# A mixture-of-experts kernel on one core: the first chunk as eight plain products instead of seven products of sum forms

## The chip, the cores and the metric

The kernel runs on one core of a Trainium2 chip. The metric is device time in microseconds for one execution, and lower is better. Engines are named as in the profile: PE (TensorE, matrix products), DVE (VectorE), ACT (ScalarE), POOL (GpSimd) and SP (SyncE, which here only issues DMAs).

## The reference, cut to what matters

```python
# x: (16, 256, 256) float32;  Wg, Wu: (8, 256, 1024);  Wd: (8, 1024, 256);  Sg, Su, Sd: the shared expert
g = einsum('bsd,edf->ebsf', h, Wg);  u = einsum('bsd,edf->ebsf', h, Wu)
expert_outs   = einsum('ebsf,efd->ebsd', silu(g) * u, Wd)
expert_output = einsum('be,ebsd->bsd', gating_probs, expert_outs)
shared = einsum('bsf,fd->bsd', silu(h @ Sg) * (h @ Su), Sd)
out = x + (1 - sg) * expert_output + sg * shared
```

So there are nine experts (eight routed, one shared) over 4096 tokens of width 256, with a hidden width of 1024, all in float32.

## The kernel before, in words

**Tiles and groups.** The tokens are cut into 8 tiles of 512. Two tiles (t = 0 and 1) make a group, and there are four groups. For each group the kernel walks through 9 experts with 8 chunks of 128 hidden units each. `n` counts the chunks of the first group. The input of a group has four blocks: x[c][t], with c the half of the width and t the tile. A chunk has four weight blocks of 128x128: A11 and A12 (gate weights, first and second half of the width), A21 and A22 (up weights), and the down weights D0 and D1.

**Seven products instead of eight.** Gate and up for two tiles are a 2x2 times 2x2 block product, which takes eight block products if done plainly. The kernel makes it with seven, p1 to p7, from sums of weight blocks (S1 to S4) and sums of input blocks (T1 to T4). The raw slot of A21 is overwritten by S3. In the first group p1 opens the bank `chain_ps`, p6, p7 and p4 add to it, p5 and p3 use `p53_ps`, p2 uses `side_ps`. Between them ACT copies banks away ("taps": tap1, tap5, tap_u2) and DVE adds the taps to banks to form gate0, gate1 and up1; up0 is what p4 leaves in `chain_ps`. ACT then applies silu, and DVE multiplies silu, up and a coefficient to h0 and h1.

**hi and lo.** Each operand is split into hi (ACT casts it to the matmul's format) and lo (raw minus hi), and each product is three matmuls: hi by hi, hi by lo, lo by hi (`product`, L680 to L686). So one product is three rows of the trace, of lines L684, L685 and L686.

**The first group makes the weights.** In group 0, for each chunk, SP loads the raw blocks, POOL makes the sums (`weight_sums`, L457), ACT the hi part (`weight_hi`, L975), POOL the lo part (`weight_lo`, L480, 1152 columns), and SP stores both to DRAM (`keep_gate`, `keep_down`), from where the later groups fetch them. The down weights of two chunks also get sums (`pair_sums`, four additions, and `down_lo`). There are four raw slots: chunk 4 takes the slot of chunk 0, and ACT may write the hi part of chunk 4 only when the four stores of chunk 0 have landed (`kept_stored[0]`, L982).

**The order on the engines.** Each engine has one program, in order. For the first group, PE's is `first_units` (chunks 0 and 1, then the down product of chunk 0 for tile 1), and then `unit(e, k)` per chunk: p4 of the chunk before, p1, p5, down products of tile 0, p6, p2, p3, p7, down products of tile 1. That is 11 products. The other engines follow with units of their own. ACT's unit ends with both silus and, in the first expert, with the hi part of a chunk further on (`both_hi`: chunk 3 behind unit 1, chunk 4 behind unit 2, chunk 5 behind unit 3). At the head of its next unit stands the hi part of h1. POOL runs through `first_chunks` (L571) in a written order: the sums of chunks 1, 2 and 3, the lo parts of chunks 1 and 2, the pair sums, the lo part of chunk 3, the sums of chunk 4, `down_lo`, the lo part of chunk 4, the pair sums of 2 and 3, the sums of chunk 5. SP runs through `first_keeps` (L305).

**The opening of chunk 0.** In the kernel before, DVE makes the four sums of chunk 0 (`w_sum`, L1419) and the lo parts of its blocks and of all seven input forms (`first_forms`, L1402). ACT makes the hi parts in `first_unit` (L1148). Then `first_steps` (DVE) and `second_unit` (ACT) bring in chunk 1.

## Time and profile before

| quantity | us |
|---|---|
| median of 3 runs | 2104.42 |
| lowest, highest | 2104.19, 2104.86 |
| profiled execution, its own time | 2105.31 |
| its span (first to last instruction) | 2103.5 |
| PE busy | 2091.9 (99%) |
| POOL busy | 1611.3 (77%) |
| DVE busy | 1447.7 (69%) |
| ACT busy | 1304.2 (62%) |

The busy shares are means over the whole span. The change touches the first chunk only, which lies within the first 25 us or so. The later stages run the same instructions in both kernels.

### The profile page before, as it was taken

To read this page: it belongs to the slowest core of one execution; us is meant where nothing else is said; L and a number is where in the kernel's file an instruction comes from. 1 tells how busy PE (TensorE), PEld (TensorE's weight loads), DVE (VectorE), ACT (ScalarE), POOL (GpSimd) and SP (SyncE) were. 2 spreads that over 40 slices of the span, in tenths; PEclk is the share of its full clock that TensorE was granted. 3 is DMA by queue.
4 is the path that set the end of the run, shared out by engine and by line. 5 is a ranking of instruction groups with operands and counts; after the bars stand their busy time and mean duration, and the time that the engine had idled before them with its cause. 6 is when DMAs were issued, how large, how long until landed. Compare 5 with 4: busy or idle time off the path is not lost.

```text
span 2103.5 us, 33963 instructions
## 1 busy us (share of the span) xinstructions
PE 2091.9 (99%) x9183; PEld 1719.2 (82%) x9183; DVE 1447.7 (69%) x2630; ACT 1304.2 (62%) x2335; POOL 1611.3 (77%) x1442
## 2 busy tenths in 40 slices
PE   8999999999999999999999999999999999999999
PEld 6888888888888888888888888888888888888887
DVE  7666666666666666666676666666667666666666
ACT  7777777777566555555556655555555555555555
POOL 7988887877488777777778877777777778777776
PEclk9999999999999999999999999999999999999999
DMA  6976666666555455445445446445445445545443
GB/s 221 349 245 238 234 242 230 242 229 232 203 197 209 173 215 209 173 194 209 174 193 210 177 191 229 178 188 209 180 186 210 184 184 210 203 183 209 183 183 143
DMA packets 122747, 433.94 MB, mean 206 GB/s; under 512 B 13760, under 2 KB 41792, under 8 KB 122688
## 3 DMA queue, kind: packets, MB, share of 16 engines
q1 hardware_dynamic: 122688, 433.32, 54.9%
q8 instruction: 17, 0.28, 0.1%
q14 instruction: 42, 0.34, 0.0%
HBM read 329.85 MB, written 103.28 MB: 206 GB/s over the span
## 4 chain that ended last, share of the span: by engine, by line
PE 99%; DVE 1%; issue 0%; ACT 0%; DMA 0%; DVEq 0%; ACTq 0%
PE chain_ps L684 15%; PE chain_ps L685 15%; PE chain_ps L686 15%; PE down_ps L686 8%; PE down_ps L685 8%; PE down_ps L684 8%; PE p_ps L684 6%; PE p_ps L686 6%; PE p_ps L685 6%; PE side_ps L686 4%; PE side_ps L685 4%; PE side_ps L684 4%; DMA acc<-xT 0%; ACT h_forms L1089 0%; DVE acc L1232 0%
## 5 line engine op out<-in xcount | busy, mean ns | idle before, releaser
L455 POOL TENSOR_TENSOR h_forms<-h_t,h_forms 128x512 fp32r<-128x512 f32 x429 | 560.5, 1325 | 269.1 <-ACT h_forms L1089 269.1
L684 PE MATMUL chain_ps<-x_hi,gate_forms 128*128 128x512 f32 x1080 | 422.5, 391 | 0.2
L686 PE MATMUL chain_ps<-x_hi,gate_forms 128*128 128x512 f32 x1080 | 420.7, 390 | 0.0
L685 PE MATMUL chain_ps<-x_lo,gate_forms 128*128 128x512 f32 x1080 | 420.7, 390 | 0.0
L455 POOL TENSOR_TENSOR h_t<-h_b,h_t 128x512 f32<-128x512 f32 x214 | 312.1, 1458 | 73.5 <-DVE h_b L1226 58.2
L1232 DVE TENSOR_TENSOR p_ps<-tap_p,chain_ps 128x512 f32<-128x512 f32 x216 | 150.4, 696 | 247.5 <-PE chain_ps L686 247.5
L1103 ACT COPY chain_ps<-chain_ps 128x512 f32<-128x512 f32 x216 | 123.1, 570 | 281.6 <-DVE h_a L1226 193.9
L1089 ACT CAST h_forms<-h_t 128x512 fp32r<-128x512 f32 x429 | 267.3, 623 | 15.1 <-POOL h_t L455 3.6
L455 POOL TENSOR_TENSOR w_lo<-w_raw,w_hi 128x1152 fp32r<-128x1152 f32 (+2 forms) x74 | 191.9, 2594 | 78.1 <-ACT w_hi L984 77.6
L684 PEld LDWEIGHTS chain_ps<-x_hi,gate_forms 128*128 128x128 f32 x1080 | 202.5, 188 | 54.8 <-ACT chain_ps L1103 5.3
L686 PEld LDWEIGHTS chain_ps<-x_hi,gate_forms 128*128 128x128 f32 x1080 | 202.7, 188 | 43.2
L685 PEld LDWEIGHTS chain_ps<-x_lo,gate_forms 128*128 128x128 f32 x1080 | 202.8, 188 | 37.3
L1108 ACT ACTIVATE silu<-chain_ps 128x512 f32<-128x512 f32 x216 | 129.5, 599 | 161.7 <-PE chain_ps L686 161.7
L1232 DVE TENSOR_TENSOR silu<-tap_p,chain_ps 128x512 f32<-128x512 f32 x216 | 148.0, 685 | 80.2 <-PE chain_ps L686 80.2
L1089 ACT CAST h_forms<-h_b 128x512 fp32r<-128x512 f32 x214 | 134.2, 627 | 109.2 <-DVE h_b L1226 109.2
L1030 ACT COPY tap_p<-p_ps 128x512 f32<-128x512 f32 x288 | 170.7, 593 | 6.3
L455 POOL TENSOR_TENSOR h_t<-h_a 128x512 f32<-128x512 f32 x108 | 140.2, 1298 | 44.5 <-DVE h_a L1226 44.5
L1093 ACT ACTIVATE p_ps<-p_ps 128x512 f32<-128x512 f32 x216 | 125.7, 582 | 72.5 <-PE p_ps L686 72.4
L686 PE MATMUL down_ps<-h_forms,down_forms 128*128 128x512 f32 x433 | 168.7, 390 | 0.0
L684 PE MATMUL down_ps<-h_forms,down_forms 128*128 128x512 f32 x433 | 168.5, 389 | 0.0
L685 PE MATMUL down_ps<-h_forms,down_forms 128*128 128x512 f32 x433 | 168.5, 389 | 0.0
L684 PE MATMUL p_ps<-x_hi,gate_forms 128*128 128x512 f32 x432 | 168.2, 389 | 0.0
(117 smaller groups left out, 4878.0 us busy)
## 6 DMA issues: line engine op xcount, KB each, us to landing
gate_forms<-kept_gate SPq DMA_DIRECT2D x216, 896.0 KB, 7.4
down_forms<-kept_down SPq DMA_DIRECT2D x108, 896.0 KB, 4.6
kept_gate<-w_hi SPq DMA_DIRECT2D x72, 448.0 KB, 2.5
kept_gate<-w_lo SPq DMA_DIRECT2D x72, 448.0 KB, 3.1
w_raw<-w SPq DMA_DIRECT2D x72, 256.0 KB, 3.0
w_raw<-w SPq DMA_DIRECT2D x72, 128.0 KB, 2.8
kept_down<-d_hi SPq DMA_DIRECT2D x36, 256.0 KB, 2.3
kept_down<-d_lo SPq DMA_DIRECT2D x36, 256.0 KB, 2.8
```

The source lines that it names most:

```text
L455: return nc.gpsimd.tensor_tensor(dst, a, b, ALU.subtract)
L684: nc.tensor.matmul(bank, w_high, hi, start=start, stop=False, **on)
L685: nc.tensor.matmul(bank, w_high, lo, start=False, stop=False, **on)
L686: return nc.tensor.matmul(bank, w_low, hi, start=False, stop=stop, **on)
L1030: nc.scalar.copy(tap_p5[:], p53_ps[:]).then_inc(p5_tapped, 1)
L1089: nc.scalar.copy(h_forms[:, H_AT[form]], h_full[form][:] if full is None else full).then_inc(form_hi[form], 1)
L1093: nc.scalar.activation(p53_ps[:], p53_ps[:], ACT.Silu).then_inc(silu_done[1], 1)
L1103: nc.scalar.copy(chain_ps[:, 1 - k % 2, :], chain_ps[:, k % 2, :]).then_inc(p1_seeded, 1)
L1108: nc.scalar.activation(silu[:, 0], chain_ps[:, 1 - k % 2, :], ACT.Silu).then_inc(silu_done[0], 1)
L1232: return nc.vector.tensor_tensor(dst, a, b, ALU.add)
```

## The change

Chunk 0 is computed by eight plain products (`plain_chunk` on PE): gate0, up0, gate1 and up1 are each two products accumulated in one bank, in the order gate0, up0, gate1, up1 with the first half of the width, then gate1, up1, gate0, up0 with the second. Its gate and up come out of the banks directly, so chunk 0 has no taps and no additions, and ACT reads both silus from the banks. The fourth input block (x[0][1], called b12) gets a hi and a lo part of its own, in the place of a form of the second group. The sums S1 to S4 of chunk 0, which are still needed for the copies in DRAM, are made on POOL; their hi part (a DVE copy) and lo part (DVE) come at the end of DVE's `first_steps`. Chunk 1 is then the first with taps and forms. The lo part of chunk 1's A11 and A12 moves from POOL to DVE. POOL makes the coefficients before the lo part of chunk 1. SP's `first_keeps` loads chunk 5 first, then 6, then 4, and the store of chunk 0's down weights moves behind the loads of the down weights of chunks 4 and 5, which wait for the pair sums (`d_sums` 4).

```diff
-FIRST_X_HI = (B11, T1, B21, B22, T2, T3, T4)
+FIRST_X = (B11, B21, B22, T1, T2, T3, T4)
+PLAIN = 1
@@ SP, first_keeps
-                sp.wait_ge(w0_lo_done, 4)
-                load_blocks(0, 4)
-                sp.wait_ge(w_lo_done, 1)
-                load_blocks(0, 5)
-                keep_gate(0, 0)
-                keep_down(0, 0)
-                sp.wait_ge(w_lo_done, 2)
-                load_blocks(0, 6)
-                sp.wait_ge(w1_lo_done, 2)
+                sp.wait_ge(w_lo_done, 1)
+                sp.wait_ge(w1_gate_lo_done, 1)
+                load_blocks(0, 5)
+                sp.wait_ge(w_lo_done, 2)
+                load_blocks(0, 6)
+                sp.wait_ge(w0_lo_done, 4)
+                load_blocks(0, 4)
+                keep_gate(0, 0)
+                sp.wait_ge(w1_lo_done, 1)
                 sp.wait_ge(d_sums, 4)
                 load_down(0, 4)
                 load_down(0, 5)
+                keep_down(0, 0)
                 keep_gate(0, 1)
@@ POOL
             def first_chunks():
+                plain_chunk_sums()
                 next_sums(0, 0)
-                pool.wait_ge(w1_hi_done, 1)
-                part_lo(1, A11, A12).then_inc(w1_lo_done, 1)
+                coefficients()
                 pool.wait_ge(w_hi_done, 1)
                 part_lo(1, S3, S4).then_inc(w_lo_done, 1)
-                coefficients()
                 next_sums(0, 1)
                 next_sums(0, 2)
+                pool.wait_ge(w_hi_done, 2)
+                part_lo(2, D0, A22)
                 pool.wait_ge(w_hi_done, 3)
-                part_lo(2, D0, A22)
+                part_lo(2, S1, S4).then_inc(w_lo_done, 1)
                 pool.wait_ge(w_hi_done, 4)
-                part_lo(2, S1, S4).then_inc(w_lo_done, 1)
                 part_lo(1, D0, D1).then_inc(w1_lo_done, 1)
                 pair_sums(0, 0)
@@ PE
+            def plain_chunk():
+                gate0, up0, gate1, up1 = chain_ps[:, 1, :], chain_ps[:, 0, :], p53_ps[:], side_ps[:]
+                first_w(0)
+                b11 = x_of(0, B11, True)
+                product(gate0, made(0, A11), b11, start=True, stop=False)
+                first_w(1)
+                product(up0, made(0, A21), b11, start=True, stop=False)
+                pe.wait_ge(b12_lo_done, 1)
+                b12 = x_hi[:, 1, B11, :], x_lo[:, 1, B11, :]
+                product(gate1, made(0, A11), b12, start=True, stop=False)
+                product(up1, made(0, A21), b12, start=True, stop=False)
+                b22 = x_of(0, B22, True)
+                product(gate1, made(0, A12), b22, start=False, stop=True).then_inc(p3_done, 1)
+                product(up1, made(0, A22), b22, start=False, stop=True).then_inc(p7_done, 1)
+                b21 = x_of(0, B21, True)
+                product(gate0, made(0, A12), b21, start=False, stop=True).then_inc(p2_done, 1)
+                product(up0, made(0, A22), b21, start=False, stop=True).then_inc(p4_done, 1)
             def first_units():
-                (p1, p5, p2, p6, p3, p7 of chunk 0, and its p4 behind p5 of chunk 1)
+                plain_chunk()
                 p1_of(1, 1)
                 p5_of(1, 1)
                 p6_of(1, 1)
...
@@ ACT, the new first_units in the place of first_unit and second_unit
                 x_form_hi(0, B11)
                 act.wait_ge(w_loaded[0], 16)
                 first_w_hi(A11, A12)
+                first_w_hi(A21, A22)
+                act.wait_ge(x_loaded[1][0], 16)
+                nc.scalar.copy(x_hi[:, 1, B11], acc[:, 1, 0, :]).then_inc(b12_hi_done, 1)
+                x_form_hi(0, B21)
+                x_form_hi(0, B22)
                 x_form_hi(0, T1)
                 act.wait_ge(w_loaded[1], 16)
                 second_w_hi(A11, A12, w1_hi_done)
                 x_form_hi(0, T2)
                 x_form_hi(0, T3)
+                x_form_hi(0, T4)
+                act.wait_ge(d_loaded[0], 16)
+                first_w_hi(D0, D1)
                 act.wait_ge(w_sums, 4)
                 second_w_hi(S3, S4, w_hi_done)
+                (silu of gate1 from p53_ps, silu of gate0 from chain_ps)
+                h1_hi_of(0)
                 tap1(1, 1)
                 tap5(1)
                 weight_hi(0, 2, 0)
                 tap_u2_of(1, 1)
                 weight_hi(0, 2, 1)
                 h0_hi_of(0, 0)
+                (D0, D1 of chunk 1, silu_of(1, 1), silu_of(0, 1), both_hi(3))
@@ DVE, first_forms and first_steps
                 x_lo_of(B11)
                 w_lo_of(A11, A12, 1)
-                (four w_sum)
+                w_lo_of(A21, A22, 2)
+                dve.wait_ge(b12_hi_done, 1)
+                minus(x_lo[:, 1, B11], x[0][1], x_hi[:, 1, B11].bitcast(F32)).then_inc(b12_lo_done, 1)
                 x_sum_of(0, x[0][1], x[0][0])
+                x_lo_of(B21)
+                x_lo_of(B22)
                 x_sum_of(1, x[1][1], sums[0])
                 x_sum_of(2, x[1][1], x[0][1])
+                minus(lo_of(1, A11, A12), raw_of(1, A11, A12), hi_of(1, A11, A12).bitcast(F32)).then_inc(w1_gate_lo_done, 1)
                 x_sum_of(3, x[1][0], sums[1])
+                (x_lo_of T1, T2, T3; h1_made(0, 0); x_lo_of T4; then h1_lo_of(0), h0, w_lo_of(D0, D1, 3))
                 gate1(1)
                 gate0(1)
                 up1_made(1, 1)
                 h0_lo_of(0, 0)
                 h1_made(0, 1)
+                dve.wait_ge(w0_sums, 4)
+                nc.vector.tensor_copy(hi_of(0, S3, S4), raw_of(0, S3, S4)).then_inc(w0_hi_done, 1)
+                w_lo_of(S3, S4, 4)
```

All waits on counters that chunk 0 no longer advances (taps, gate0, gate1, up1, p1, p5, p6) are lowered by `PLAIN`.

## Rows read from the trace of the kernel before

**Rows 1.** The page's head and its first part: busy time of each engine.
```profile
span 2103.5 us, 33963 instructions
PE 2091.9 (99%) x9183; PEld 1719.2 (82%) x9183; DVE 1447.7 (69%) x2630; ACT 1304.2 (62%) x2335; POOL 1611.3 (77%) x1442
```

**Rows 2.** Timeline of PE: start, duration, line, operands.
```profile
5.23 0.79 PE L684 MATMUL chain_ps<-x_hi,w_hi 128*128 128x512 f32 x1 [5.23 <-DVE w_lo L1235]
...
22.33 0.50 PE L684 MATMUL chain_ps<-x_hi,w_hi 128*128 128x512 f32 x1 [0.31 <-DVE side_ps L1232]
...
37.45 0.39 PE L684 MATMUL chain_ps<-x_hi,w_hi 128*128 128x512 f32 x1
```

**Rows 3.** Chain that ended last, pieces in order: start, length, what.
```profile
8.98 0.43 PE p_ps L685
...
14.93 0.23 PE chain_ps L685
```

**Rows 4.** Timeline of POOL, 8 to 20 us.
```profile
8.40 2.41 POOL L460 TENSOR_TENSOR w_raw<-w_raw 128x128 f32<-128x128 f32 x4 [7.93 <-DMA w_raw<-w]
11.95 1.75 POOL L455 TENSOR_TENSOR w_lo<-w_raw,w_hi 128x640 fp32r<-128x640 f32 x1
14.51 3.66 POOL L460 TENSOR_TENSOR w_raw<-w_raw 128x128 f32<-128x128 f32 x8
18.13 1.84 POOL L455 TENSOR_TENSOR w_lo<-w_raw,w_hi 128x768 fp32r<-128x768 f32 x1
18.13 3.69 POOL L455 TENSOR_TENSOR w_lo<-w_raw,w_hi 128x768 fp32r<-128x768 f32 x3
```

**Rows 5.** Timeline of DVE, 11 to 21 us.
```profile
11.27 0.68 DVE L1235 TENSOR_TENSOR down_ps<-acc,down_ps 128x512 f32<-128x512 f32 x1
11.87 0.41 DVE L1235 TENSOR_TENSOR w_lo<-w_raw,w_hi 128x256 fp32r<-128x256 f32 x1
18.20 2.05 DVE L1235 TENSOR_TENSOR w_lo<-w_raw,w_hi 128x256 fp32r<-128x256 f32 x1
```

**Rows 6.** Timeline of ACT, 8 to 12 us.
```profile
8.24 0.63 ACT L1010 CAST x_hi<-acc 128x512 fp32r<-128x512 f32 x1
11.13 0.74 ACT L1146 CAST w_hi<-w_raw 128x640 fp32r<-128x640 f32 x1
```

**Rows 7.** Timeline of SP's queue, and one issue's time to landing.
```profile
20.28 0.80 SPq L272 DMA_DIRECT2D w_raw<-w  x2
22.90 1.37 SPq L292 DMA_DIRECT2D kept_down<-w_lo  x1
...
kept_down<-w_lo SPq DMA_DIRECT2D x1, 64.0 KB, 3.6
```

**Rows 8.** Timeline of ACT, 29 to 39 us.
```profile
29.40 1.23 ACT L984 CAST w_hi<-w_raw 128x768 fp32r<-128x768 f32 x2
30.53 0.58 ACT L1020 CAST h_hi<-side_ps 128x512 fp32r<-128x512 f32 x1
...
37.01 1.25 ACT L984 CAST w_hi<-w_raw 128x768 fp32r<-128x768 f32 x2
```

**Rows 9.** Timeline of POOL, 23 to 37 us.
```profile
23.57 2.69 POOL L455 TENSOR_TENSOR w_lo<-w_raw,w_hi 128x1152 fp32r<-128x1152 f32 x1
28.01 1.30 POOL L455 TENSOR_TENSOR d_lo<-d_raw,d_hi 128x512 fp32r<-128x512 f32 x1
30.70 2.67 POOL L455 TENSOR_TENSOR w_lo<-w_raw,w_hi 128x1152 fp32r<-128x1152 f32 x1 [1.40 <-ACT w_hi L984]
35.14 1.84 POOL L460 TENSOR_TENSOR w_raw<-w_raw 128x128 f32<-128x128 f32 x4
```

**Rows 10.** Timeline of DVE, 34 to 43 us.
```profile
34.93 0.69 DVE L1232 TENSOR_TENSOR gate<-tap_p,side_ps 128x512 f32<-128x512 f32 x1 [0.92 <-PE side_ps L686]
36.29 0.70 DVE L1232 TENSOR_TENSOR side_ps<-tap_p,chain_ps 128x512 f32<-128x512 f32 x1
42.41 0.69 DVE L1232 TENSOR_TENSOR gate<-tap_p,side_ps 128x512 f32<-128x512 f32 x1 [0.29 <-PE side_ps L686]
```

More of the change, by code:

```diff
@@ L753, in p2_of @@
             def p2_of(n, k):
-                after(pe, h_lo_done[1], n)
-                opening = isinstance(n, int) and n == 0
-                product(side_ps[:], made(k % SLOTS, A12), x_of(0, B21, opening), start=True, stop=True).then_inc(p2_done, 1)
+                pe.wait_ge(h_lo_done[1], n)
+                product(side_ps[:], made(k % SLOTS, A12), x_of(0, B21, False), start=True, stop=True).then_inc(p2_done, 1)
             def p3_of(n, k):
-                pe.wait_ge(p5_tapped, n + 1)
-                opening = isinstance(n, int) and n == 0
+                pe.wait_ge(p5_tapped, n + 1 - PLAIN)
                 product(
-                    p53_ps[:], made(k % SLOTS, S4), x_of(0, B22, opening), start=False, stop=True, goes_on=True
+                    p53_ps[:], made(k % SLOTS, S4), x_of(0, B22, False), start=False, stop=True, goes_on=True
                 ).then_inc(p3_done, 1)
             def p7_of(n, k):
-                pe.wait_ge(u2_tapped, n + 1)
-                opening = isinstance(n, int) and n == 0
-                if opening:
-                    first_w(2)
+                pe.wait_ge(u2_tapped, n + 1 - PLAIN)
+                opening = isinstance(n, int) and n == 1
                 product(
@@ L795, in unit @@
                 n = group(0, e, k)
-                p4(0, (k - 1) % CHUNKS, n - 1)
+                p4(0, (k - 1) % CHUNKS, n - 1, first=isinstance(n, int) and n == 2)
                 p1_of(n, k)
@@ L905, in p5 @@
                     if opening and k == 0:
-                        pe.wait_ge(gate1_done, n)
+                        pe.wait_ge(gate1_done, n - PLAIN)
                     else:
@@ L1100, in seed @@
                 def seed(n, k):
-                    act.wait_ge(p1_done, n + 1)
+                    act.wait_ge(p1_done, n + 1 - PLAIN)
                     act.wait_ge(h0_done, n)
@@ L1246, in h1_made @@
                 dve.wait_ge(silu_done[1], n + 1)
-                dve.wait_ge(up1_done, n + 1)
+                if isinstance(n, int) and n == 0:
+                    dve.wait_ge(p7_done, 1)
+                else:
+                    dve.wait_ge(up1_done, n + 1 - PLAIN)
                 weighed(side_ps[:], silu[:, 1], side_ps[:], 0, e, 1, h1_done)
@@ L1400, in two_groups, with w_lo_of @@
                     tap(7, gp, pc - 1, is_first(ep, jp))
+            def w_lo_of(first, last, parts):
+                dve.wait_ge(w0_hi_done, parts)
+                minus(lo_of(0, first, last), raw_of(0, first, last), hi_of(0, first, last).bitcast(F32)).then_inc(
+                    w0_lo_done, 1
+                )
             def first_forms():
```

157 lines of the change are left out of this document (66 added, 91 removed).

## The prediction

> **What bounds the kernel now.** I read the page first: PE is busy for 2091.9 of 2103.5 us, and no other engine is over 77% [rows 1]. So only what PE waits for, or how much PE has to do, can move the time. Then PE's timeline. Its first matmul starts at 5.23, and the unit of chunk 2 (unit 2) starts at 22.33, the last time it is shown waiting at such a point, for DVE's up1 [rows 2]. From there PE runs on without a gap worth naming: unit 4 starts at 37.45 [rows 2]. Per unit that is 11 products of three matmuls at 0.227 us, 7.48 us. The whole question is therefore how many microseconds earlier or later PE arrives in that gapless stretch, and whether it stays gapless. What PE loses before it is never won back, since PE has no slack later.
>
> The chain of waits gives PE's two paces. A matmul took 0.43 us at 8.98 and 0.23 at 14.93 [rows 3]: 512 columns at 1.2 and at 2.4 GHz. A product thus costs 1.28 us in the slow opening and 0.68 after it.
>
> **PE's own work.** Chunk 0 has 8 products in the place of 7. Up to unit 2 that makes 16 (8, 6 of chunk 1, 2 down) in the place of 15, so +0.68 at the fast pace, +1.28 at the slow one. Against it stands idle time. From 5.23 to 22.33 are 17.10 us. If the pace rises where it does in the rows of before, near 14.1, the 45 matmuls of before need (14.1 - 5.23 - 1.70)/0.427 = 17 slow ones (1.70 is the gap after p1 while DVE makes sums) and 28 fast ones, 6.35 us. That ends at 20.45, and 1.9 us were waits in the fast part. The new 48 matmuls without any wait would be 21 slow and 27 fast: 5.23 + 8.9 + 6.1 = 20.2. If the pace rises as long after 5.23 as it did after the steady run that began at 8.2, that is at 11.1, it is 14 and 34: 18.9. So PE alone could gain 2.1 to 3.4 us. The rest of the working asks who lets it.
>
> **Who feeds chunk 1.** Product p5 of chunk 1 needs POOL's lo part of its S3 to S4. The steps before that:
> - POOL makes the four sums of chunk 0 from 5.5 on, 1.84 us for four (half of eight in 3.66 [rows 4]), and ends before the raw blocks of chunk 1 are there at 8.4 [rows 4]. They cost nothing, except that they meet DVE. The four sums of chunk 1 follow, 2.41 as before, to 10.8; the coefficients (0.9) to 11.7.
> - ACT must first cast b12 (its block is issued third and lands near 5.9), B21, B22 (8.24 in the rows [rows 6], now 7.8 at the earliest), T1, A11/A12 of chunk 1, T2, T3, T4, D0/D1, and only then S3 to S4 of chunk 1, which took 0.74 [rows 6]. T4 is the last sum of DVE.
> - DVE works in steps of 0.60 us (11.27 to 11.87 [rows 5]). From the T1 cast (8.7 to 9.3): x_sum 1 to 9.9, x_sum 2 to 10.5, the lo part of A11/A12 (0.35), x_sum 3 to 11.5. Then on ACT T4 12.1, D0/D1 12.4, S3 to S4 13.1. POOL's lo part of 640 columns took 1.75 [rows 4], at the least 1.6: done at 14.75.
> - Contention. In the rows, DVE's 256 columns took 2.05 us at 18.20 and 0.41 at 11.87 [rows 5]. At 18.20 POOL was inside an instruction of 1.84 us from 18.13 [rows 4], and DVE's ended 0.28 after it. Both read two operands from SBUF. POOL's four sums at 8.40 took 2.41, not 1.84, beside DVE's work: 0.57 lost. In the new order six DVE instructions of that kind lie beside POOL's eight sums. Nothing is the lower end, 0.46 each (2.8 in all) the upper. I take 0.1 each, 0.6 us, because POOL lost 0.14 per instruction in the rows. So POOL's lo part is done at 15.35.
>
> PE's chunk 0 ends at 13.4 (early pace) or 14.8 (late pace), and p1 of chunk 1 needs the silu of gate0, which stands on ACT behind that same S3 cast: 14.8 to 15.0. p5 then starts at 15.5 to 15.7 in either case. So the extra product and the pace of PE hardly matter (0.25 us between the two). From 15.6: p5, p6, p3, p2 to 18.3. p7 needs tap_u2, which stands on ACT behind the hi part of chunk 2, and that needs POOL's sums to 17.2: cast 0.8, tap 0.6, so p7 at 18.6. Two down products, and unit 2 could start at 20.7. Its p1 needs chunk 2's lo part from POOL: 15.35 + 3.66 (eight sums) + 0.3 for meeting DVE + 1.84 + 0.9 = 22.0. Before, that p1 started 0.81 behind 22.33, at 23.14. **Gain at this point: 1.1 us.**
>
> **What comes due behind it.** The added DVE copy and lo part of S3 to S4 (640 columns each, about 0.8 by the 0.41 for 256) are issued near 22.1, in front of the lo part of h1 for unit 2. The trace shows no such copy within SBUF. Beside POOL's small additions it costs 0.4 at the low end (a faster copy, no wait). Behind POOL's 2.69 us instruction [rows 9] it costs 3. I take 2.2 to 2.9 for the pair, ending near 24.9, since POOL is then in its lo part of D0/D1 and in the pair sums. POOL, in turn, ends the pair sums at 22.0 + 0.7 + 1.84 + 1.3 (DVE's two) = 25.8; before it ended them at 23.6, where the 2.69 us instruction starts [rows 9].
>
> The Trainium skill bears on this copy: the page "SBUF — State Buffer", section "Who interferes with whom", says that a VectorE copy in a two-port mode, or an instruction with two SBUF inputs, and a GpSimd instruction that reads SBUF exclude each other for the whole instruction. For the copy no run here shows it. For two inputs the 2.05 us agrees. Without the rule for the copy, everything behind it would come 0.4 to 0.7 us sooner.
>
> SP: the load of chunk 4 and the four stores of chunk 0 start when DVE's last lo part is done, and the down store also waits for the pair sums. Before, these DMAs began at 20.28, the last of them was issued at 22.90 and landed 3.6 later, at 26.5 [rows 7], early enough. Now the last one is issued behind two down loads: 25.8 + 0.9 + 0.8 = 27.5 or later, landed at 31.1 at most, 30.9 taken. ACT may not write the hi part of chunk 4 before it. Before, ACT did that at 29.40 [rows 8]. Call the new time T = 30.9 (POOL's sums of chunk 4 are due at 30.3, so they don't decide).
>
> From T two paths lead to PE.
> - h1's hi part stands behind it: T + 1.13 in the place of 30.53 [rows 8], 1.5 late. Until PE, there is DVE's idle time of 0.92 before gate0 and 0.46 between the end of up1 (36.29 + 0.70 [rows 10]) and p4 at 37.45 [rows 2], less 0.05 for the signal: slack 1.33. PE's unit 4 starts 0.2 later than before.
> - POOL's lo part of chunk 4 waits for ACT: T + 1.25 = 32.15 in the place of 30.70 [rows 9], 1.45 late. POOL's queue runs on from there without idle time: pair sums, then sums of chunk 5, which ended at 35.14 + 1.84 = 36.98 [rows 9], right before ACT's cast of chunk 5 at 37.01 [rows 8]. That cast moves 1.45 too. Slack to gate0 of the next unit: 0.29 [rows 10] + 0.41. PE loses 1.45 - 0.70 = 0.75.
>
> Behind unit 5 DVE has its 0.92 again before gate0, and I find no further loss. **Sum: 0.75 us later than before.** The gain of 1.1 is used up by the later stores and sums. On the profiled execution this is 2105.31 + 0.75 = 2106.06, of which 2103.5 + 0.75 is span and 1.81 lies around it. That execution was 0.89 above the median of the runs shown, so against the median: 2104.42 + 0.75 = 2105.17, **2105.2 us**.
>
> Edits that cost nothing: the `PLAIN` offsets, the wait on x_lo in p4 of unit 2 (all input forms are done near 16), the coefficients' new place (0.9 us while ACT still casts; without that cover it would be 0.9 on the path), chunk 5's load ahead of chunk 4's.
>
> **Rivals.**
> - *The gain stays.* If DVE and POOL hardly meet and the copy is short, POOL's lo part of chunk 1 is done at 14.75, the pair sums end near 24.0, T falls to 29.4 or less, and both paths have slack. Then the gain at p1 of chunk 2 remains, 1.1 + 0.6, up to 2.1: 2102.3 to 2103.3. For it: POOL's sums fit before 8.4, and no idle time is shown before the cast at 29.40. Against it: 18.20's 2.05 us.
> - *A POOL instruction of 2.69 us cuts in.* If DVE's lo part of S3 to S4 is asked for once POOL has begun the lo part of chunk 3, it waits up to 2.7 us. Then h1's lo part, the load of chunk 4 and the stores all come 2.7 later. T is 33.6, and PE loses 0.75 + 2.7: 2107.9. It decides from the point where DVE's lo part starts after POOL's last pair sum. I have 24.1 against 25.5, a margin of 1.4.
> - *The pace of PE alone decides.* The early rise gives 18.9 for unit 2, a gain of 3.4: 2101.0. Against it: the waits for POOL above.
>
> **How the numbers follow.** Forecast (0.75 later, between 0.8 earlier and 2.2 later, by 0 to 1.3 us more contention than taken or less) 0.55: 2103.6 to 2106.6. The gain stays: 0.25. The long POOL instruction: 0.15. PE's pace: 0.05. The range 2102.9 to 2107.2 leaves out the upper part of the gains and the rival of 2107.9. A change of 0.2%, 4.2 us, is about what a measurement of this kernel can tell from no change. Only contention beyond the second rival reaches that on the slow side (0.04), and on the fast side only PE's pace at its best (0.02).
>
> **What would show it.** Right: PE starts the product p1 of chunk 2 between 21.3 and 22.8; the lo part of chunk 1's S3 to S4 on POOL ends at 15.3; the down store of chunk 0 is the last SP issue before ACT's cast of chunk 4, which starts after 30 with an idle time before it; DVE's gate0 of units 3 and 4 has lost its wait for PE, and PE shows a wait at p4 there. Wrong: that cast at 29 or before, or PE gapless from 22 on with the start of unit 4 before 37.

## The result, and the profile after

The changed kernel took 2108.24 us (median of 21 executions, 2105.82 to 2110.55). The kernel before took 2104.42 on the same chip (21 executions, 2103.92 to 2105.85). The ratio is 1.0018, 95% interval 1.0012 to 1.0024: 3.8 us slower. That is less than the 0.2% (4.2 us) which the forecast took for the least that can be told from no change, but the interval leaves out 1, and the time is outside the range of the forecast. Two things must be explained: 3.8 us, and the spread, 4.7 us against 1.9.

The profiled execution took 2110.02 (span 2108.2). It is one of the slowest of the changed kernel, 1.8 above its median; the one of before was 0.9 above its own. So its account explains the tail first, and the experiments have to say what the median owes to it.

The page's head answers to [rows 1]: three matmuls more, 1.8 us more of busy PE, and 4.7 us more span. So PE also waited more.

```profile
span 2108.2 us, 33852 instructions
PE 2093.7 (99%) x9186; PEld 1720.8 (82%) x9186; DVE 1447.4 (69%) x2626; ACT 1301.9 (62%) x2332; POOL 1613.5 (77%) x1445
```

PE's waits (total, times, longest us). The first is there before too [rows 2]. Two are new, and the four others of before, 2.2 us in all between 8 and 22.4 us, are gone.

```profile
PE chain_ps L702 <- DVE w_lo L1255: 5.2, 1, 5.2
PE chain_ps L702 <- ACT tap_p L1060: 3.0, 1, 3.0
PE chain_ps L702 <- ACT silu L1196: 2.1, 1, 2.1
```

The windows of the changed kernel (stretch; then busy us and instruction count of PE, PEld, DVE, ACT and POOL; granted clock, DMA share, GB/s) show where: 10 to 20 and 30 to 40 us. In both the granted clock is down as well.

```profile
10.00:20.00 10.00, 7.90 (x28) 6.04 (x27) 7.86 (x15) 7.29 (x14) 8.27 (x15) 0.83 0.19 64
...
30.00:40.00 10.00, 7.04 (x26) 5.40 (x25) 3.42 (x7) 4.25 (x8) 5.82 (x8) 0.83 0.90 317
```

The same two windows of the kernel before read 1.00. For 10 to 20 us the column misleads: the matmuls of before still lie 0.43 us apart until 14.3 us, the pace of 1.2 GHz, and in the changed kernel that pace ends at 8 us and comes back from 14.76 to 18.4.

```profile
10.00:20.00 10.00, 9.79 (x33) 6.95 (x31) 9.43 (x15) 8.44 (x17) 9.74 (x17) 1.00 0.16 56
...
30.00:40.00 10.00, 10.00 (x46) 8.29 (x45) 6.30 (x13) 7.62 (x15) 7.78 (x10) 1.00 0.90 308
```

The chain that ended last, through the later stretch (start, length, what), tells the whole story:

```profile
22.94 0.74 DVE w_hi L1483
23.71 0.98 DVE w_lo L1255
24.70 0.33 SPq L276
...
28.62 4.94 DMA kept_down<-w_lo
...
34.82 0.58 ACT h_hi L1045
35.39 0.49 ACT tap_p L1060
35.93 0.80 PE chain_ps L702
36.73 0.43 PE chain_ps L703
...
39.12 0.24 PE p_ps L703
```

DVE's late copy and lo part of chunk 0's S3 to S4 release SP. SP issues loads and stores, and the last store of chunk 0's down weights lands 4.94 us after its issue. Only then may ACT overwrite that buffer with chunk 4's hi part. On SP, ACT and PE the same stretch reads as follows (start, duration, line, operands, idle time before and who ended it). SP's queue, which answers to [rows 7]:

```profile
25.07 0.43 SPq L288 DMA_DIRECT2D kept_gate<-w_hi  x1
...
26.09 1.97 SPq L280 DMA_DIRECT2D w_raw<-w  x2
28.09 0.49 SPq L296 DMA_DIRECT2D kept_down<-w_hi  x1
28.62 0.46 SPq L296 DMA_DIRECT2D kept_down<-w_lo  x1
```

The DMA view of that last issue, us to landing at its end:

```profile
kept_down<-w_lo SPq DMA_DIRECT2D x1, 64.0 KB, 4.9
```

ACT, which answers to [rows 8]:

```profile
33.67 1.24 ACT L1009 CAST w_hi<-w_raw 128x768 fp32r<-128x768 f32 x2 [4.39 <-DMA kept_down<-w_lo]
34.82 0.58 ACT L1045 CAST h_hi<-side_ps 128x512 fp32r<-128x512 f32 x1
35.29 0.59 ACT L1060 COPY tap_p<-chain_ps 128x512 f32<-128x512 f32 x1
```

PE, which answers to [rows 2] and [rows 3]:

```profile
14.76 0.62 PE L702 MATMUL chain_ps<-x_hi,w_hi 128*128 128x512 f32 x1 [2.10 <-ACT silu L1196]
...
32.59 0.39 PE L704 MATMUL down_ps<-h_hi,w_lo 128*128 128x512 f32 x1
35.93 0.80 PE L702 MATMUL chain_ps<-x_hi,w_hi 128*128 128x512 f32 x1 [2.96 <-ACT tap_p L1060]
...
41.49 0.39 PE L702 MATMUL chain_ps<-x_hi,w_hi 128*128 128x512 f32 x1
```

The rows at 29.40 of before and 33.67 of after are the same cast, 4.27 us later. PE's unit 4 starts at 41.49 in place of 37.45, 4.04 later. That is made of: PE was 0.6 ahead at unit 3 (29.40 in place of 29.98); it then had no matmul for 3.1 us; and behind that gap the matmuls lie 0.43 apart, the pace of 1.2 GHz, until 38.9, which is some 6.7 of them at 0.2 too much, 1.35. Sum 3.9. The last 0.7 of the 4.7 of span come later, and not by the change: as much and more lies between executions of one kernel. The second trace of the kernel before (set 3 below) shows it best. It is 0.79 ahead of the first at unit 5, still 0.78 ahead at 529 us, and then falls back bit by bit, with no wait on PE over 0.2 us, to end 0.39 behind. The same two matmuls, in the first trace of before and then in the second:

```profile
529.09 0.39 PE L684 MATMUL chain_ps<-x_hi,w_hi 128*128 128x512 f32 x1
...
2099.15 0.39 PE L686 MATMUL down_ps<-h_forms,down_forms 128*128 128x512 f32 x1
```

```profile
528.31 0.39 PE L684 MATMUL chain_ps<-x_hi,w_hi 128*128 128x512 f32 x1
...
2099.54 0.39 PE L686 MATMUL down_ps<-h_forms,down_forms 128*128 128x512 f32 x1
```

The time of an execution less its start of unit 5 lies between 2060.4 and 2061.8 us over all eighteen traces, for both kernels alike. What makes this 1.4 us isn't known. It blurs what one profiled time says of the opening.

### The profile page after: what moved, and what is told of

Read it like the earlier page. It is cut to its first block, busy times and chain, and to the rows that moved or that the text cites. A ratio compares the mean times of both kernels' runs of the same rounds, so it can differ in the third digit from the quotient of the medians.

```text
span 2108.2 us, 33852 instructions
## 1 busy us (share of the span) xinstructions
PE 2093.7 (99%) x9186; PEld 1720.8 (82%) x9186; DVE 1447.4 (69%) x2626; ACT 1301.9 (62%) x2332; POOL 1613.5 (77%) x1445
## 4 chain that ended last, share of the span: by engine, by line
PE 98%; DVE 1%; DMA 0%; issue 0%; ACT 0%; SPq 0%; DVEq 0%; ACTq 0%
PE chain_ps L702 15%; PE chain_ps L704 15%; PE chain_ps L703 15%; PE down_ps L704 8%; PE down_ps L702 8%; PE down_ps L703 8%; PE p_ps L702 6%; PE p_ps L703 6%; PE p_ps L704 6%; PE side_ps L704 4%; PE side_ps L703 4%; PE side_ps L702 4%; DMA kept_down<-w_lo 0%; DMA acc<-xT 0%; DVE down_ps L1255 0%
```

## Experiments

Four sets, each on one chip and with the kernel before (33 executions in each; 11 of every experiment). Its medians were 2105.05, 2105.24, 2104.33 and 2104.21, so only differences within a set are used. The ratios' intervals are some 0.0018 wide, about 3.9 us. Most single steps below are smaller than that, so the traces carry them, and medians support them where several agree.

### Set 1: is it the late store, the late lo part, or SP's order?

Store first:

```diff
                 load_blocks(0, 4)
                 keep_gate(0, 0)
+                keep_down(0, 0)
                 sp.wait_ge(w1_lo_done, 1)
                 sp.wait_ge(d_sums, 4)
                 load_down(0, 4)
                 load_down(0, 5)
-                keep_down(0, 0)
```

> The changed kernel, but the store of chunk 0's down weights stands right behind the store of its gate weights again, ahead of the wait for the pair sums and of the two down loads. Theory A (the landing of that store, at 33.57 us in the changed kernel, holds ACT's cast of chunk 4, and PE's 2.96 us gap and the slow clock behind it follow from that): the last store is issued near 26.9 and lands near 31; the down load of chunk 4 goes out later than in the changed kernel and lands near 31.3, and the same cast waits for it too. ACT's wait falls from 4.39 to about 2.2, PE's gap from 2.96 to about 0.8, the clock does not fall behind it: about 2104.8 median. Theory B (the order of the stores is incidental; POOL's sums of chunk 4, done at 29.6, and DVE's added copy set the cast): ACT's wait ends where POOL ends, and the time stays at 2107.5 to 2108.5. Theory C (the loss is the fall of the clock behind PE's early 2.10 us gap): that gap is untouched, time stays at 2108.

Copy and lo part of S3 to S4 early on DVE:

```diff
                 w_lo_of(D0, D1, 3)
+                dve.wait_ge(w0_sums, 4)
+                nc.vector.tensor_copy(hi_of(0, S3, S4), raw_of(0, S3, S4)).then_inc(w0_hi_done, 1)
+                w_lo_of(S3, S4, 4)
                 gate1(1)
...
-                dve.wait_ge(w0_sums, 4)
-                nc.vector.tensor_copy(hi_of(0, S3, S4), raw_of(0, S3, S4)).then_inc(w0_hi_done, 1)
-                w_lo_of(S3, S4, 4)
```

> The changed kernel, but DVE makes the copy and the lo part of chunk 0's S3 to S4 ahead of gate1 of chunk 1, into its idle time of 1.73 us there, not at the end of first_steps. Theory A: the load of chunk 4 and the gate stores leave near 22 in the place of 25, the down stores still behind the pair sums, near 25.3, and land near 29.5 to 30. ACT's cast waits under 1 us, PE has no gap at chunk 3, the clock stays up: 2103.7 to 2104.3 median. Theory B (POOL's load decides): POOL's pair sums end only 0.7 earlier, so the cast moves by 0.7 and the time is near 2107. Theory C: unchanged at 2108. A mishap that is possible: the lo part meets POOL's 1.84 us instruction and gate1 of chunk 1 comes up to 1.3 late, then 2105.

Both edits:

> Both edits, the store order and the early lo part. Theory A: the last store of chunk 0 is issued near 23.5 and lands before 28, the down load of chunk 4 near 28.5: ACT's cast starts behind its silus at 29.2 without a wait, PE runs gapless from 14.8 on and arrives at chunk 4 about 0.6 us ahead of the kernel before: 2103.8 median. Theory B: near 2107. Theory C: 2108.

The kernel before with its down store behind the loads, as the change has it:

```diff
                 keep_gate(0, 0)
-                keep_down(0, 0)
...
                 load_down(0, 4)
                 load_down(0, 5)
+                keep_down(0, 0)
```

> The kernel before, with only the store of chunk 0's down weights moved behind the two down loads of chunks 4 and 5 (and the load of chunk 6). Theory A: the landing of the last store moves from 26.5 to about 30, 0.6 behind ACT's cast at 29.40, within the slack of 1.3 us to PE: 2104.4, no change. So the order alone costs nothing, and it takes the late lo part of chunk 0 as well. If the order of the stores alone were the cause (rival), this kernel loses 3 us or more: 2107.5.

Measured (before 2105.05): store first 2106.99 (2106.35 to 2107.33; ratio 1.0009, 1.0000 to 1.0018); lo early 2106.34 (1.0007, 0.9998 to 1.0016); both 2106.22 (1.0005, 0.9996 to 1.0015); before with the late store 2105.28 (1.0001, 0.9992 to 1.0010).

In all three variants of the changed kernel the tail is gone: none of their executions lies above 2107.4, but for a single one of 4301. SP's order by itself costs nothing that can be told (0.2), since in the kernel before its lo parts are done early. So the order hurts only together with the late lo part, as the forecast had it. But none gets back to before: 2103.7 to 2104.8 were expected, from 0.7 below the kernel before to 0.4 above, and 1.2 to 1.9 above were measured. ACT's waits in store first show that the late store had companions (total, times, longest us): the load of chunk 4 is now what comes last, and POOL's sums of chunk 5 are late behind it. The first line counts the whole run; its longest, 1.2, is the wait before the cast of chunk 5.

```profile
ACT w_hi L1009 <- POOL w_raw L465: 3.0, 7, 1.2
...
ACT w_hi L1009 <- DMA w_raw<-w: 1.7, 1, 1.7
```

In this trace PE is 0.93 ahead of [rows 2] at unit 4 and 0.28 at unit 5, against the 44.94 of before. The 0.65 between the two is the forecast's second path, which it priced at 0.75.

### Set 2: the clock, and the changed kernel once more

The changed kernel, unchanged:

> The changed kernel itself, on the chip of the next three, for comparison. If the loss is one wait of ACT for a store and the clock that falls behind PE's gap in some executions and not in others, its trace shows the same wait of about 4.4 us, and its times spread over some 4 us while those of the kernel before spread over less than 2: median 3.5 to 4 us above the kernel before.

The changed kernel with 13 matmuls by a tile of zeros in the gap of unit 3 (`fill` makes them in this edit and in the next two; POOL sets the tile ahead of its first sums):

```diff
                 down0((k - 2) % CHUNKS, start=isinstance(n, int) and n == 2, stop=False)
+                if isinstance(n, int) and n == 3:
+                    fill(down_ps[:, 0, 1, :], x_hi[:, 0, B11, :], 13, False)
                 p6_of(n, k)
```

> The changed kernel with 13 more matmuls of zero weights (they add zeros to a down bank) on PE where it waits at chunk 3, 2.95 us of work in a gap of 3.11. Nothing is made earlier. Theory A with the clock as its second part: PE is at work in the gap, the clock stays at 2.4 GHz, and the 1.35 us that the matmuls behind the gap lose at 1.2 GHz come back: median 1.0 to 1.4 us below the changed kernel, and a narrower spread. If the wait alone is the loss and the clock counts for nothing: the same as the changed kernel, or 0.1 to 0.3 more, since the filler may end behind the wait.

Both edits of set 1, and five such matmuls behind the last product of the plain chunk:

```diff
-                product(up0, made(0, A22), b21, start=False, stop=True).then_inc(p4_done, 1)
+                product(up0, made(0, A22), b21, start=False, stop=False)
+                fill(up0, b21[0], 5, True).then_inc(p4_done, 1)
```

> The kernel with both edits (store first, lo part early), and 5 matmuls of zero weights at the end of the plain chunk, 1.1 us of work in the gap of 0.9 to 2.1 us before p1 of chunk 1. Theory (the early gap lets the clock fall for 3.4 us in some executions, which costs up to 1.7 us when nothing behind it waits for DMA): median 0.3 to 0.8 below the kernel with both edits (2106.2 on its chip, 1.2 above the kernel before), spread smaller. Rival (PE is held by DVE and POOL behind chunk 1 in any case): the same time.

The kernel before with four such matmuls behind its first product:

```diff
-                product(chain_ps[:, k % 2, :], made(s, A11), x_of(0, B11, opening), start=True, stop=True).then_inc(p1_done, 1)
+                moving = x_of(0, B11, opening)
+                last = product(chain_ps[:, k % 2, :], made(s, A11), moving, start=True, stop=not opening)
+                if opening:
+                    last = fill(chain_ps[:, k % 2, :], moving[0], 4, True)
+                last.then_inc(p1_done, 1)
```

> The kernel before with 4 matmuls of zero weights behind its first product, in the gap of 1.70 us (1.7 us of work at the slow pace). The clock should rise between 8.6 and 12 us in the place of 13.4 to 14.3, so that some ten matmuls run at 0.227 in the place of 0.427 us: PE has 1 to 2 us less to do before chunk 2. Theory (PE's pace is the bound of the opening): 1 to 1.5 us faster than the kernel before. Rival (DVE and POOL feed chunk 1, as the working before the result has it; PE's pace is hidden): within 0.3 us of the kernel before.

Measured (before 2105.24): changed again 2107.20 (2106.02 to 2109.99; 1.0012, 1.0002 to 1.0021); gap filled 2108.91 (2108.42 to 2109.98, one of 6136 apart; 1.0017, 1.0008 to 1.0027); both and filler 2106.12 (1.0004, 0.9995 to 1.0013); before with filler 2106.99 (2105.62 to 2109.11; 1.0007, 0.9998 to 1.0017).

The changed kernel is 2.0 above its kernel before here, not 3.8 as in the first measurement (and 2.3 in the fourth set); 3.5 to 4 were expected.

The second trace of the changed kernel comes from an execution of 2106.02 us, 4 us faster than the first. SP issued the same store 0.55 sooner, and it landed much sooner:

```profile
28.07 0.43 SPq L296 DMA_DIRECT2D kept_down<-w_lo  x1
```

Its landing, and then ACT:

```profile
kept_down<-w_lo SPq DMA_DIRECT2D x1, 64.0 KB, 2.3
```

```profile
30.43 1.25 ACT L1009 CAST w_hi<-w_raw 128x768 fp32r<-128x768 f32 x2 [1.74 <-DMA kept_down<-w_lo]
```

Its PE waits 0.3 for tap_p, not 3.0, and its clock doesn't fall. So the landing, 2.3 in one execution and 4.9 in another, goes with most of the spread of the changed kernel. Why it differs isn't known. The third trace (set 4, 2106.23 us) landed after 2.3 as well, and there ACT's cast starts almost where the forecast had it, at 30.9. Its ACT and PE:

```profile
30.82 1.25 ACT L1009 CAST w_hi<-w_raw 128x768 fp32r<-128x768 f32 x2 [1.77 <-DMA kept_down<-w_lo]
```

```profile
33.09 0.50 PE L702 MATMUL chain_ps<-x_hi,w_hi 128*128 128x512 f32 x1 [0.28 <-ACT tap_p L1060]
```

Its unit 4 starts at 37.40 and its unit 5 at 45.55, which is 0.05 earlier and 0.61 later than in the trace of [rows 2]. The forecast had 0.2 and 0.75 later for this cast.

With the gap filled, the store was late again, and the filler lay where the gap was. PE, and then ACT:

```profile
32.00 3.19 PE L712 MATMUL down_ps<-x_hi,zeros 128*128 128x512 f32 x13
35.03 0.39 PE L705 MATMUL chain_ps<-x_hi,w_hi 128*128 128x512 f32 x1
```

```profile
32.31 1.25 ACT L1020 CAST w_hi<-w_raw 128x768 fp32r<-128x768 f32 x2 [4.07 <-DMA kept_down<-w_lo]
```

PE goes on at 0.23 per matmul, and this unit, from start to start, takes 10.52 us (28.59 to 39.11) where it took 12.09 in the trace of after (29.40 to 41.49), with a wait on ACT that differs by 0.3 only. The fall of the clock thus costs about what the rows gave, 1.3 to 1.6. My expectation of the median failed all the same: the filler costs 3.0 in every execution, and the wait that it covers is long in a part of them only. The clock's share belongs to that part too: the execution at the median of the first measurement, 2108.24, has a mean granted clock of 1.000.

Filling the opening gives nothing that can be told (0.9 above its set's kernel before, where both edits alone were 1.2 above theirs; in the traces PE is 0.3 ahead of [rows 2] at unit 3, and 0.5 without the filler), and in the kernel before it costs 1.75: the filler delays p1's signal, and ACT and DVE behind it. There the pace rises by 11.35 and not at 14.3, and still nothing is gained: PE then waits 1.98 us for DVE at 15.04. So the pace of the first chunk isn't what bounds the opening. A fall behind the gap before chunk 1 does count for something. Among the traces in which the lo part of S3 to S4 stays late, the three that have one start p1 of chunk 2 at 22.4 to 22.8 with no wait in front of it. Five without one start it at 21.6 to 22.1, behind a wait of 0.3 for POOL.

### Set 3: the load and the store both early

The kernel before, unchanged:

> The kernel before, unchanged, for a second trace of it. The prediction was worked out from one execution that was 0.89 us above the median; in its trace DVE's 256 columns at 18.20 took 2.05 us because POOL's 768 columns had started 0.07 us earlier. If that explains the 0.89: here DVE comes first, its instruction takes 0.4 to 0.5 us, PE starts chunk 2 near 21.1 and not at 22.33. Rival: that execution was slow for another reason, and PE starts chunk 2 at 22.3 here too.

The changed kernel with its down store as soon as the lo part of D0 and D1 is there, ahead of the load of chunk 4:

```diff
                 load_blocks(0, 6)
+                sp.wait_ge(w0_lo_done, 3)
+                keep_down(0, 0)
                 sp.wait_ge(w0_lo_done, 4)
...
                 load_down(0, 5)
-                keep_down(0, 0)
```

> The changed kernel with one edit: the two stores of chunk 0's down weights leave as soon as their lo part is done (near 22, behind chunk 6's load), ahead of the wait for the lo part of S3 to S4. Nothing on DVE, POOL, ACT or PE is moved. Theory A (the last store's landing, 2.3 to 4.9 us behind its issue at 28, is the loss and the spread): the last things that ACT's cast of chunk 4 needs are now the gate stores, landing near 29.4, and the down load, near 29.5 to 30.3. ACT waits 0.4 to 1.2 us, PE has no gap over 0.5 us, the median is 0.2 to 0.5 above the kernel before and the spread under 1.5 us, against 4 of the changed kernel. Rival (anything else in the change): median 2 us above the kernel before and the spread stays.

Both edits of set 1, and the silu of gate0 first on ACT:

```diff
                 x_form_hi(0, T4)
-                act.wait_ge(d_loaded[0], 16)
-                first_w_hi(D0, D1)
+                act.wait_ge(p2_done, 1)
+                nc.scalar.activation(silu[:, 0], chain_ps[:, 1, :], ACT.Silu).then_inc(silu_done[0], 1)
...
-                act.wait_ge(p2_done, 1)
-                nc.scalar.activation(silu[:, 0], chain_ps[:, 1, :], ACT.Silu).then_inc(silu_done[0], 1)
+                act.wait_ge(d_loaded[0], 16)
+                first_w_hi(D0, D1)
```

> The kernel with both edits of before (store first, lo part early), and on ACT the silu of gate0 ahead of the cast of chunk 1's S3 to S4, the silu of gate1 behind it and the D0/D1 cast last. PE's p1 of chunk 1 can start near 13.4 and not near 14.5. If PE is bound by its early gap: 0.7 us faster than that kernel, 0.4 above the kernel before. If DVE bounds it (it has the 640 columns of lo in front of gate1, and PE waits 0.7 us for up1 at chunk 2): no gain, 1.0 to 1.2 above the kernel before.

The early down store and that silu:

> The early down stores and the silu of gate0 first. The version that should be nearest to what the plain chunk can give: p5 of chunk 1 near 15.6 in the place of 16.0, no store on the path. 0 to 0.3 us above the kernel before, or equal to it. If the extra product itself costs (0.68 us of PE, gapless afterwards), it stays 0.4 or more above.

Measured (before 2104.33): before again 2104.24 (0.9998, 0.9989 to 1.0007); early down store 2105.65 (2104.76 to 2106.68; 1.0006, 0.9997 to 1.0015); both and silu 2105.97 (1.0007, 0.9998 to 1.0016); down store and silu 2105.75 (1.0007, 0.9998 to 1.0016).

The early down store is 1.3 above its kernel before, with a spread of 1.9; 0.2 to 0.5 and under 1.5 were expected. In its trace ACT's cast of chunk 4 waits 1.17 for POOL's sums, and for no store.

Moving the silu gives nothing. It brings p1 of chunk 1 forward, from 14.55 to 13.44, and the next product waits in its place (PE's waits of the last of the four):

```profile
PE p_ps L703 <- POOL w_lo L461: 1.2, 1, 1.2
PE chain_ps L703 <- ACT silu L1191: 0.7, 1, 0.7
```

The second trace of before shows that I had worked from an unlucky opening, but not that this made the execution slow: without the 2.05 us it took 2105.71, more than the first with its 2105.31, for it lost its lead behind 529 us. The instruction that took 2.05 at 18.20 [rows 5] takes 0.42 there, and PE's unit 2 starts 0.8 sooner than at 22.33. DVE, and then PE:

```profile
18.37 0.42 DVE L1235 TENSOR_TENSOR w_lo<-w_raw,w_hi 128x256 fp32r<-128x256 f32 x1
```

```profile
21.54 0.50 PE L684 MATMUL chain_ps<-x_hi,w_hi 128*128 128x512 f32 x1
```

In the trace of before with the late store it took 0.47, and PE was 1.2 ahead. So the 2.05 us is one outcome of three that I have, and the worst.

### Set 4: the same with the changed kernel beside it, and the copy moved

> The changed kernel once more, beside the next three on one chip. 2 to 4 us above the kernel before, spread near 4 us, from the landing of chunk 0's last store.

> The early down stores again, now on the same chip as the changed kernel. If the landing of that store is what the changed kernel lost and what spread its times: spread of 2 us or less and a median 0.7 to 2.5 below the changed kernel's, 1.3 above the kernel before as on the other chip. If the 1.3 there was a matter of the chip: the same as the changed kernel here.

The early down store, and chunk 0's S3 to S4 copied by ACT:

```diff
                 tap1(1, 1)
+                act.wait_ge(w0_sums, 4)
+                act.wait_ge(p4_done, 1)
+                act.wait_ge(w0_lo_done, 2)
+                first_w_hi(S3, S4)
                 tap5(1)
...
-                dve.wait_ge(w0_sums, 4)
-                nc.vector.tensor_copy(hi_of(0, S3, S4), raw_of(0, S3, S4)).then_inc(w0_hi_done, 1)
                 w_lo_of(S3, S4, 4)
```

> The early down stores, and the hi part of chunk 0's S3 to S4 made by ACT (640 columns, 0.73 us, in its idle time of 0.69 before tap5 of chunk 1) and not by DVE at the end of first_steps. With the early down stores alone PE lost 0.58 us between chunks 3 and 5, because POOL's sums of chunk 5 came late for ACT's cast (two waits of 1.2 us). Theory (DVE's copy holds POOL back, 0.72 and 0.93 us in the place of 0.46 for the pair sums beside it): POOL's pair sums end 0.5 to 0.9 earlier, that loss shrinks to 0.1 or less, and the median is 0.4 to 0.6 below the early down stores alone, 0.8 above the kernel before. Rival (the rest is the extra product and the order of chunk 1): no change.

That copy on ACT, the lo part ahead of gate1 on DVE, and SP's order of the kernel before but for the load of chunk 5, which stays first:

> ACT makes the hi part of S3 to S4 of chunk 0 before tap5 of chunk 1, DVE its lo part before gate1 of chunk 1, and SP has the order of the kernel before (load of chunk 4, all four stores of chunk 0, then the load of chunk 6). The stores leave near 18.5. ACT and POOL wait for no store or load. If then DVE's added 0.97 us is covered by its idle 0.74: 0 to 0.4 above the kernel before, spread 1.5 us; if gate1 comes 0.4 late, as with the early lo part before: 0.8 above.

Measured (before 2104.21):

| kernel | median | lowest to highest | ratio (95%) |
|---|---|---|---|
| changed | 2106.50 | 2105.54 to 2110.22 | 1.0013 (1.0004 to 1.0022) |
| early down store | 2105.39 | 2105.01 to 2106.43 | 1.0005 (0.9996 to 1.0014) |
| and copy by ACT | 2105.62 | 2105.04 to 2106.05 | 1.0007 (0.9998 to 1.0016) |
| all early | 2105.64 | 2105.37 to 2105.85 | 1.0007 (0.9998 to 1.0016) |

Two of eleven executions of the changed kernel are at 2109.6 and 2110.2; in the first measurement seven of 21 were at 2109.6 or above, and those seven alone had a mean granted clock of 0.998. Without the late store no execution is there, and the spread falls from 4.7 to 1.4, 1.0 and 0.5. The median falls by 1.1, as expected for the early down store. The copy by ACT adds nothing to that (0.4 to 0.6 less were expected), so nothing shows DVE's copy as the cause of the rest. The last kernel has no late store, no late load and nothing on ACT that waits over 0.7 for POOL, and still takes 1.4 more than the kernel before (0 to 0.8 were expected). In its trace PE waits in the opening (total, times, longest us):

```profile
PE chain_ps L702 <- ACT silu L1196: 1.4, 1, 1.4
PE chain_ps L702 <- POOL w_lo L460: 0.6, 1, 0.6
```

It reaches unit 5 0.5 ahead of the trace of [rows 2]. The others with the store or the lo part out of the way are between 0.05 behind (both and silu) and 0.78 ahead there, and the further trace of before and the one of before with the late store 0.79 and 1.22 ahead. So in these traces the plain chunk gets PE into the gapless stretch no sooner than before does.

## Why the prediction was wrong

**What bounds the kernel.** Right in that PE waits for nothing over 0.2 us from unit 5 on in any trace, so what the change does to PE's waits is done by then. But up to 1.2 us between executions of one kernel come behind 529 us, so an execution's own time says little of its opening.

**The opening, "the extra product and the pace of PE hardly matter".** Right for the steps that feed chunk 1: POOL's lo part ends at 15.25 (15.35 forecast), and p1 of chunk 1 starts at 14.76 (14.8 to 15.0), though the plain chunk ended at 12.7, sooner than either pace of the forecast had it. Unit 2's p1 starts at 22.57 (22.0 forecast, inside its own bounds), but behind no wait: there PE's own pace decides, slow again behind the gap of 2.10. In the second trace, without that fall, it is 22.11, behind POOL, as forecast. These are POOL and DVE of the changed kernel:

```profile
13.71 1.54 POOL L460 TENSOR_TENSOR w_lo<-w_raw,w_hi 128x640 fp32r<-128x640 f32 x1 [1.48 <-ACT w_hi L1171]
...
22.86 0.47 POOL L460 TENSOR_TENSOR d_raw<-w_raw 128x128 f32<-128x128 f32 x1
23.28 0.72 POOL L460 TENSOR_TENSOR d_raw<-d_raw,w_raw 128x128 f32<-128x128 f32 x1
24.07 0.93 POOL L460 TENSOR_TENSOR d_raw<-w_raw,d_raw 128x128 f32<-128x128 f32 x1
24.96 2.68 POOL L460 TENSOR_TENSOR w_lo<-w_raw,w_hi 128x1152 fp32r<-128x1152 f32 x1
```

```profile
22.85 0.82 DVE L1483 CAST w_hi<-w_raw 128x640 fp32r<-128x640 f32 x1
23.71 0.97 DVE L1255 TENSOR_TENSOR w_lo<-w_raw,w_hi 128x640 fp32r<-128x640 f32 x1
```

**"Gain at this point: 1.1 us."** Right in one trace, wrong in its base. Against the execution with the 2.05 us lock it was 0.6 (23.14 to 22.57), and 1.0 in the second trace (22.11). But p1 of chunk 2 starts at 22.34 in the second trace of before and at 21.92 in the one with the late store: against these the gain is 0.2 at the best, or a loss. The forecast set a change's one outcome against one outcome of before, and took that wait, itself a matter of who asks first, for a fixed part of the kernel.

**The step that failed: "27.5 or later, landed at 31.1 at most, 30.9 taken".** The mechanism and the place were right: this cast, this store, this order of SP's queue. The sizes were not. The pair sums ended at 25.00, 0.8 sooner than worked out. SP's two down loads took 1.97 to issue, not 0.9, and stood behind two gate stores at 25.07 and 25.55 which I had let pass as done. The last store was issued at 28.62, 1.1 late, and landed 4.9 later, not 3.4. T was 33.67. Where the same store landed after 2.3 us, T was 30.43 and 30.82, and with the latter PE came out as forecast (0.61 late at unit 5, 0.75 forecast). "At most" stood on a single landing time [rows 7]; the same DMA landed after 2.3 in two other executions. The 4.94 us are a wait of 4.39 on ACT.

**"From T two paths lead to PE."** There is a third. ACT's tap_p, the second instruction behind the cast and its copy of h1, feeds product p6 of the running unit 3. It reaches PE 2.3 behind T (33.67 to 35.93; in the third trace 30.82 to 33.09). At T = 30.9 that is 33.2, where it costs PE little: a wait of 0.28 in the third trace. At 33.67 it is the first to bite: PE stood from 33.0 to 35.9. The sign named in the forecast, a wait at p4, came at p6. A bound on T should have been carried down every path behind the cast, as the range was meant to hold the late end.

**Left out: the clock.** Behind a gap of 3.1 us the matmuls go at 1.2 GHz until 38.9, 1.35 us lost, about the amount that the filler confirms. I had treated the pace as a matter of its one rise, and no term or rival had a fall in it. The Trainium skill, "TensorE: Matmul & The Clock Gate", "Part 1: The HAM clock gate", says that the default state is throttled and that activity lifts it. The rows behind 35.93 agree: the pause brought the slow state back.

**The second path, 0.75.** Right in size where it can be seen: 0.7 between units 4 and 5 in store first and in the second and third traces of the changed kernel. PE's wait there is for tap_p again, at p6 of unit 4. With the copy on ACT it vanished, yet PE came to unit 3 0.9 later than with the early down store alone. That trace has the slow pace from 14.83 to 19.6, and the other has not.

**The rivals.** "A POOL instruction of 2.69 us cuts in" named T = 33.6 and 2107.9, nearly what was seen, by another cause: POOL's long instruction began at 24.96, behind DVE's pair, which ended at 24.68. The forecast had that order. By its own measure, DVE's lo part against POOL's last pair sum, the margin was 1.25 (23.71 to 24.96), near the 1.4 forecast (which counted to 25.5, though its sum gives 25.8). The number came true by the road of SP's queue and the landing. "The gain stays" fell with its base. "PE's pace alone decides" fell too: the pace rose at 8 us, sooner than that rival asked, and unit 2 started at 21.89, not at 18.9.

**What the median owes to it.** In the fourth set the late store is worth 1.1 of 2.3 us. The first measurement had 3.8, and no experiment ran in that one, so how it splits is not measured; if the same 1.2 to 1.4 are in it, 2.4 to 2.6 are the store's. The other 1.2 to 1.4 (0.9 to 1.9 over all sets), common to the plain chunk's variants with the store or the lo part out of the way, isn't settled. Each by itself is within its interval or at its edge, but all ten are on the same side. Their traces reach unit 5 on average 0.4 ahead of [rows 2], before's three (with the late store's) 0, 0.8 and 1.2 ahead, 0.7 on average: 0.3 apart, too little. But two of those three profiled executions of before were 0.9 and 1.5 above their medians, so the executions that make before's median may not be among them, and the differences behind unit 5, up to 1.4 between executions, are as large as what is looked for. That the opening gains nothing in these traces is shown; how much it loses, and whether by the product more or by the order on ACT and POOL, is not. None of the thirteen kernels tried against the one before, in sixteen measurements, beat it.

## What to carry to other kernels

A DMA moved to the back of a queue must be priced with its whole queue: each issue ahead of it at the length that it has right behind others (1.97 us here, against 0.82 with SP idle before them), and a landing time taken as a spread, not from one row; then carry the late end of that spread down every path behind whoever waits for the buffer. A gap on PE can be charged twice, once as the gap and once at the slow clock behind it. And where the profiled opening holds a 2 us lock, look at a second execution before counting its end as a gain, and follow the two to the end: here one lost in the long steady part more than the lock had cost the other.

## What the runs showed of the hardware

- One 64 KB store, at the same place of the same program, landed 2.3, 2.3, 4.6 and 4.9 us after its issue in four traces (the 4.6 in the kernel with the gap filled).
- The same two down loads took 1.97 us to issue at 26.09 in the changed kernel and 0.82 in the one with all early, where SP had been idle before them. In the second and third traces of the changed kernel, behind two stores again, they took 1.98 and 1.96. An issue is no constant. SP's queue in the kernel with all early:

```profile
22.52 0.34 SPq L276 DMA_DIRECT2D w_raw<-w  x1
25.05 0.82 SPq L280 DMA_DIRECT2D w_raw<-w  x2
```

- Gaps of a like size come with the slow pace or without. Behind the wait of 2.10 that ended at 14.76 PE ran at 1.2 GHz until 18.4, and the granted clock of 10 to 20 us was 0.83; so it was with waits of 2.1 (changed kernel, third trace), 1.9 (copy by ACT) and 1.8 (lo early). With another wait of 1.8 for the same silu, in the second trace of the early down store, it was 1.00.
- The Trainium skill, "SBUF — State Buffer", section "Who interferes with whom", was cited ahead for DVE's copy against POOL, with no row to show it. After has one: the pair sum of 0.72 at 23.28 lies beside the copy of 0.82, the one of 0.93 beside the two-input instruction; the free ones took 0.46. The rows agree with the rule for the copy too, and both sides paid. The copy ends 0.35 behind the pair sum that began with it (22.86 + 0.47 = 23.33, to 23.67), and the next pair sum ends 0.32 behind the copy. In the eleven other traces with that copy on DVE it likewise ends 0.35 behind the POOL instruction under way, so about 0.35 is an estimate of what it takes alone. POOL lost 0.26 and 0.47, the copy about 0.5.
- Two executions of the kernel before were 0.78 us apart the one way at 529 us and 0.39 the other way at the end, at a granted clock of 1.00 in both. Behind unit 5 the traces of all kernels here differ by up to 1.4 us, and nothing in them names the cause.
